# An RWKV layer beside attention with expert weights: a head in another order, and a tail that keeps the last pair's context on the chip

## What is computed

```python
# attention block, per batch b: x is the normalised input
pooled = x.mean(axis=1)
h = relu(pooled @ gw1.T + gb1);  logits = h @ gw2.T + gb2
top_vals, top_idx = top_k(logits, 2);  gates = softmax(top_vals)
# each of q, k, v, o: x @ Wm.T + sum over the 2 experts of gate * (x @ V.T * S) @ U.T + b
attn = softmax(q k^T)            # 16 heads of 8 channels, 1024 tokens
ctx = attn @ v
out = o-projection of ctx
# RWKV block: layer norm, token shift, k/v/r products, a scan over tokens, a second
# norm, and a squared-relu product with a sigmoid gate
```

## Time and profile before

| what | us |
|---|---|
| median of 3 runs | 449.8 |
| lowest and highest | 449.52 and 451.94 |
| the profiled execution | 448.59 |
| span of its trace, first to last instruction | 446.9 |
| busy TensorE | 421.5 |
| busy VectorE | 368.6 |
| busy ScalarE | 345.2 |
| busy GpSimd | 191.0 |

### The profile page before, as it was taken

The page is one execution under the profiler, slowest core; times in us unless marked ns, Lnnn a source line. Parts: engine busy times, 40 slices in busy tenths (PEclk is TensorE's granted clock), DMA queues, the critical chain, the costliest instruction groups (busy, mean ns, idle before and its releaser), DMA issues.

```text
span 446.9 us, 8497 instructions
## 1 busy us (share of the span) xinstructions
PE 421.5 (94%) x3223; PEld 144.1 (32%) x3224; DVE 368.6 (82%) x649; ACT 345.2 (77%) x469; POOL 191.0 (43%) x270
## 2 busy tenths in 40 slices
PE   1889989999999999999999999999999999999993
PEld 1644223333232223232323223323332333322153
DVE  8578899998999997899999789999888999950023
ACT  3547837879887898788799969778986877987862
POOL 5029581935551525282353646416265611321200
PEclk9988999999999999999999999999999999999998
DMA  7004303141414141405141413342422421010314
...
DMA packets 45661, 20.84 MB, mean 47 GB/s; under 512 B 36788, under 2 KB 36916, under 8 KB 45620
## 3 DMA queue, kind: packets, MB, share of 16 engines
...
q10 hardware_dynamic: 838, 0.69, 0.5%
...
## 4 chain that ended last, share of the span: by engine, by line
PE 84%; DVE 9%; ACT 3%; DMA 2%; issue 1%; SPq 0%; DVEq 0%
PE banks L1411 26%; PE banks L1398 22%; PE banks L1321 18%; PE banks L1366 8%; DVE half_max L1134 5%; PE banks L1283 3%; ACT probs L950 3%; PE banks L1289 1%; DMA parts<-ctx_dram 1%; PE banks L1267 1%; PE banks L1218 1%; PE banks L1454 1%; PE banks L1275 1%; PE banks L1184 1%; DVE stats L1002 1%
## 5 line engine op out<-in xcount | busy, mean ns | idle before, releaser
L1134 DVE TENSOR_REDUCE half_max<-banks 128x1 f32<-128x512 f32 x512 | 318.6, 683 | 21.2 <-PE banks L1321 19.6
L950 ACT ACTIVATE probs<-banks 128x1024 f32<-128x1024 f32 x256 | 248.2, 1023 | 47.8 <-PE banks L1398 44.6
L1411 PE MATMUL banks<-probs,v_op 128*32 128x512 f32 x1024 | 136.4, 605 | 0.6 <-ACT probs L950 0.6
L1321 PE MATMUL banks<-k_main,q_main 64*128 64x512 bf16 x512 | 117.6, 388 | 5.6 <-DVE half_max L1134 3.3
L1398 PE MATMUL banks<-q_main,k_main 64*128 64x512 bf16 x512 | 99.3, 377 | 0.4 <-ACT probs L950 0.2
L1398 PE MATMUL banks<-q_tail,k_tail 35*128 35x512 bf16 x512 | 99.3, 377 | 0.0
L1321 PEld LDWEIGHTS banks<-k_main,q_main 64*128 64x128 bf16 x512 | 36.5, 93 | 151.0 <-DVE half_max L1134 132.2
L1398 PEld LDWEIGHTS banks<-q_tail,k_tail 35*128 35x128 bf16 x512 | 27.2, 94 | 25.9
L1398 PEld LDWEIGHTS banks<-q_main,k_main 64*128 64x128 bf16 x512 | 26.4, 95 | 27.0 <-ACT probs L950 12.5
L1411 PEld LDWEIGHTS banks<-probs,v_op 128*32 128x32 f32 x1024 | 20.1, 108 | 32.7 <-issue 30.3
L696 POOL TENSOR_TENSOR work<-work 128x512 f32<-128x512 f32 x16 | 16.6, 1039 | 28.6 <-ACT work L939 28.6
...
## 6 DMA issues: line engine op xcount, KB each, us to landing
...
```

The costliest lines, as they stand in the source:

```text
L950: a.activation(probs[:, (2 * step + h) % 4, :, :], banks[:, 2 * h:2 * h + 2, :], ACT.Exp).then_inc(b_read, 1)
L1134: v.tensor_reduce(half_max[:, n % 2, u:u + 1], ring_bank(at), axis=AX.X, op=ALU.max).then_inc(a_read, 1)
L1321: mm(dst, q_main[HALF * e:HALF * (e + 1), s, P * c:P * c + P], k_main[HALF * e:HALF * (e + 1), s, CHUNK * h:CHUNK * h + CHUNK], start=True ...
L1411: last = mm(banks[g:g + 32, PV_BANK, :], v_op[:, s % 2, step, e, :], probs[:, (2 * step + h) % 4, e, :], start=(step == 0), stop=True, ski ...
```

## The change

In the head the token sums become products with a constant column (`sum_tokens`), the odd chunks are normalised on GpSimd, only batch 0's q and k weights are made at first, and the 22 casts and most of `u_s` move to GpSimd. q and k are split for banks 0 and 2 first; the work for banks 3 and 1 goes between the A units. For pair 0 `place_of` takes the units of the first 512 queries and keys first. In the tail batch 0's contexts are loaded in pair 14, all of batch 1's but the last pair's in pair 15; chunks 0 and 1 are finished inside the loop as ring jobs `out` at steps 122 and 125; the last pair goes from `ctx_sb` straight to TensorE. The reciprocals move from ScalarE to VectorE.

```diff
+FILL_JOBS = {2: [("left", 3, 1), ("project", 1)], 3: [("turn", 1)], 4: [("rows", 3)], 5: [("left", 1, 0)],
...
+OUT_JOBS = {122: 0, 125: 1}
+NORMALISED = {118: 0, 119: 1, 124: 2, 125: 3}
+EARLY = P - 2 * HD
...
+        def place_of(n, u):
+
+            if n == 0 and u < UNITS:
+                return u % 2, u // 2 % 4, u // 8
             return u % 2, u // 4, u // 2 % 2
...
+            load_pair(1, 1)
             load_tails(0, 0)
-            load_pair(1, 1)
             load_pair(2, 2)
...
+            sp.wait_ge(weff_ready, 4)
+            sp.wait_ge(zeros_ok, 1)
+            for e in range(2):
+                for h in range(2):
+                    g = 32 * (2 * e + h)
+                    sp.dma_start(w_last[g:g + HD, h, :], w_eff[EARLY + HD * e:EARLY + HD * (e + 1), 3, 1, :]
+                                 ).then_inc(last_in, 16)
...
+                if step == 0 and p == PAIRS - 2:
...
+                    load_contexts(0, HEADS)
+                if step == 0 and p == PAIRS - 1:
+                    load_contexts(1, HEADS - 2)
...
-            load_contexts(0)
-            store_ctx(PAIRS - 1, SETS - 1)
-            load_contexts(1)
...
+            def normalise(n):
+
+                pool.wait_ge(moments_ready, 4 * n + 4)
+                pool.wait_ge(rstd_ready, n // 2 + 1)
+                for i in range(4 * n, 4 * n + 4):
+                    g.tensor_scalar(xn_tok[:, i, :], x_sb[:, i, :], moments[:, i, 0:1], rstd[:, i:i + 1],
+                                    ALU.subtract, ALU.mult).then_inc(xn_in[1], 1)
...
+            pool.wait_ge(sg_ready, 1)
+            pool.wait_ge(moe_in, 16)
+            for i, b in ((2, 0), (2, 1), (3, 0), (3, 1), (0, 1), (1, 1)):
+                g.tensor_scalar(u_s[:, i, b, :], mat("qkvo"[i] + "U"), sg[:, i, b:b + 1], None, ALU.mult
+                                ).then_inc(us_ready, 1)
...
-            copy_ctx(PAIRS - 1, SETS - 1, (PAIRS - 1) // 2)
-
-            for n in range(CHUNKS):
-                act.wait_ge(attn_in[n], 32)
-                a.activation(den_T[:, n, :], den_T[:, n, :], ACT.Ln).then_inc(den_step, 1)
-                act.wait_ge(den_step, 2 * n + 1)
-                a.activation(den_T[:, n, :], den_T[:, n, :], ACT.Exp, scale=-1.0).then_inc(den_step, 1)
+            act.wait_ge(pv_done, PAIRS * 8)
+            act.wait_ge(ctx_out[1], (PAIRS - 1) // 2 * 16 + 1)
+            a.copy(ctx_sb[:, 1, :].rearrange("c (k p) -> c k p", p=P), token_tiles(bank(PV_BANK))).then_inc(ctx_copied, 1)
...
+            def normalise_ctx(n):
+
+                rows = P if n < 2 else EARLY
...
+                dve.wait_ge(attn_in[n // 2], 64)
+                v.reciprocal(den_T[0:rows, n, :], den_T[0:rows, n, :]).then_inc(recip_ready, 1)
+                dve.wait_ge(recip_ready, n + 1)
...
+            dve.wait_ge(last_den, 1)
+            for i in range(2):
+                at = slice(2 * P * i, 2 * P * (i + 1))
+                v.reciprocal(last_r[:, at], banks[:, 0, at]).then_inc(last_rec, 1)
+            for i in range(2):
+                at = slice(2 * P * i, 2 * P * (i + 1))
+                dve.wait_ge(last_rec, i + 1)
+                v.tensor_tensor(last_T[:, at], ctx_sb[:, 1, at], last_r[:, at], ALU.mult).then_inc(last_ready, 1)
+            add_out(2, bank(2))
+            add_out(3, bank(3))
...
+            def sum_tokens(n):
+
+                b = n // 2
+                pe.wait_ge(xn_in[n % 2], 4 * (n // 2 + 1))
+                for k in range(CHUNK // P):
+                    last = mm(banks[:, 4, 32 + 2 * b:34 + 2 * b], xn_tok[:, 4 * n + k, :], mean_w[:, 0:2],
+                              start=(n % 2 == 0 and k == 0), stop=(n % 2 == 1 and k == 3))
+                return last
...
+                if n == 0 and k == 0:
+                    row_free(0)
+                    row_free(2)
+                elif n == 0 and k == UNITS // 2:
+                    row_free(3)
+                elif n == 0 and k == UNITS:
+                    row_free(1)
...
+                elif name == "out":
+                    pe.wait_ge(rt_ready, 2 * q + 2)
+                    turn_rt(q, dst)
+                    project_ctx(q, dst)
...
+            turn_rt(2, bank(2))
+            turn_rt(3, bank(3))
+            pe.wait_ge(ctx_copied, PAIRS + 1)
+            for g in range(0, P, 32):
+                last = mm(banks[g:g + 32, 0, :], ident[g:g + 32, g + HD:g + HD + 1].to_broadcast([32, 32]),
+                          ctx_sb[g:g + 32, 1, :], start=True, stop=True)
+            last.then_inc(last_den, 1)
+            project_ctx(2, bank(2))
+            project_ctx(3, bank(3))
+            pe.wait_ge(last_in, 64)
+            for n in (2, 3):
+                for k in range(CHUNK // P):
+                    pe.wait_ge(last_ready, k // 2 + 1)
+                    last = mm(bank(n)[:, P * k:P * k + P], last_T[:, P * k:P * k + P], w_last[:, n - 2, :],
+                              start=False, stop=(k == 3))
                 last.then_inc(final_ps, 1)
```

380 lines of the change are left out of this document (217 added, 163 removed).

## The result

The changed kernel takes 453.97 us (median of 4 runs, 453.84 to 456.56), the kernel before 449.66 beside it: 1.0102 times as long, 95% interval 1.0076 to 1.0127. The forecast was 443.5, the range ended at 448.0. The profiled execution has 453.84 us and a span of 452.1, so 5.2 us more than before has to be found in the trace.

| stretch (us) | before | after | difference | forecast |
|---|---|---|---|---|
| to the gate's product | 14.25 | 17.71 | +3.46 | 0 |
| to the first projection | 5.85 | 6.20 | +0.35 | -1.0 |
| to the first A unit | 10.81 | 7.99 | -2.82 | -2.9 |
| opening, to the first scores | 33.72 | 37.50 | +3.78 | +0.6 |
| loop, to the last values' product | 364.30 | 368.01 | +3.71 | +3.7 |

A forecast was written before the change was run, and what follows sets the result against it. In the loop TensorE was taken as the bound, with the head shifting the loop and the tail added. Loop start -3.3, loop +3.7 and tail -6.7 made -6.3 us, from 449.8 to 443.5 us, range 442.0 to 448.0.

The forecast's parts named there:

- signs of being wrong: TensorE idling over 2 us at a time in the opening, 32 x 32 products running serially, or loop over 4 us longer.
- Three terms: Whole kernel: when the loop starts (-3.3 us), what is put into it (+3.7), how long the tail is (-6.7).
- the `out` jobs at 3.7: Loop: two inserted jobs of 1.93 us each, less at most 0.2 hidden, make it 3.7 us longer.
- Token sums: Head: 16 float32 products on TensorE at 0.24 us each, 3.9 us, priced from the o projection's row.
- Term 0: Head, to the gate's product: no gain taken, with bounds of 0.6 us earlier and 0.5 later.
- From the gate to the projection: Head: only one batch of q and k weights wanted, so about 1.0 us less, first projection at 19.1.
- From the projection to the first A unit: Head: 7.9 us in place of 10.8, first A unit at 27.0, 3.9 us earlier.
- the old bubbles were room: Opening: part of 3.2 us of new TensorE jobs fits in three bubbles of 0.88 to 0.98; 34.0 us against 33.4.
- The wait at `rows` 1: Opening: bank 1's third part stands behind `scale_shift(0)`, TensorE stands still 2 us, 1.5 us are lost.
- The rival "slower": Opening: the wait and short products keep the clock at 1.2 GHz through most of it; 452 us, chance 0.05.
- The tail: After the loop: no load in the chain, two 256-column reciprocals at the scan's 0.74 us; 6.7 us less.
- the rival "several passes": Tail: VectorE's reciprocal takes eight times an addition; gain 2.9 us smaller, 446.4, or 448.1 with slower clock; chance 0.33.

The follow-up runs named there:

- e12: e9 with the two `out` jobs inside the loop, as the changed kernel has them; median 447.08 us.
- e9: Changed kernel: VectorE normalises, ScalarE's copies sum tokens, 16 unread warm products before `rows` 1, `out` jobs behind loop, ScalarE reciprocals, denominators' product earlier; ratio 0.9898.
- e4: Changed kernel with the two `out` jobs moved from the loop to the tail; median 452.06 us, ratio 1.0027.
- e6: Changed kernel with 16 warm products, which nobody reads, filling TensorE's wait ahead of `rows` 1 in the opening; ratio 1.0030.
- e1: Changed kernel with all normalising back on VectorE, token sums still on TensorE; median 455.89 us, ratio 1.0100.
- e2: Changed kernel with normalising on VectorE and token sums back on ScalarE's copies, all chunks turned before the gate; median 452.16 us, ratio 1.0047.
- e13: e9 with 36 warm products in the opening in place of 16; 444.06 us, ratio 0.9869.
- e16: e13 with 20 in place of 32 warm products behind the gate's second product; ratio 0.9859.
- e3: Changed kernel with bank 1's third part and spread rows put ahead of `scale_shift(0)` on ScalarE; median 452.53 us, ratio 1.0057.
- e11: Kernel before with 8 and 12 warm products in two waits ahead of the first A product; ratio 0.9994.
- e15: Changed kernel with 36 warm products filling the opening's waits; ratio 1.0002.
- e7: Changed kernel with the last pair's two reciprocals made on ScalarE as Ln and Exp; ratio 1.0039.

## Why the prediction was wrong, step by step

The forecast was -6.3 us and the trace has +5.2, so 11.5 us were missed. Four steps make them up: the token sums 3.5, the way from the gate to the projection 1.35, the opening 3.2, the reciprocals of the tail 3.4. The terms for the loop and for the first A unit held. The prediction's own signs of being wrong lay elsewhere, and none of them came: TensorE idled 1.70 us at most at a time in the opening (2 was the limit), the four 32 x 32 products took 1.03 us and so ran side by side, and the loop grew by 3.71 (4 was the limit).

**What bounds it, and the loop: right.** Three terms, and the `out` jobs at 3.7 (3.71). e12 and e9 show that the jobs cost the same in the tail, once nothing waits there. What the working overlooked: with VectorE's reciprocals something does wait, and the jobs would have been cheaper in the tail (e4: nothing against this profile, 1.5 us against tails at full clock).

**Token sums: the failed step of the head.** 16 products were priced at 0.24 us each, 3.9 in all, from the o projection; they took 6.93, 0.43 each. The count was right and the row was not: it is one at TensorE's full speed, and this early TensorE ran at half of it. The head's turns tell it: four take 1.08 us at 8.35, 1.09 in the kernel before, and 0.66 in the opening at full clock (e6, at 40.69). The sums end at 17.3, ahead of the trace's first record of the clock at 22.4. A narrow product was not cheaper either: 16 instructions of two columns take 3.41 us here, and 16 of 128 columns take 3.47 in the tail at 0.50. No run has the sums at full speed, so what they would cost there is not shown. Term 0, measured +3.46; e1 and e2 show that the sums are it. GpSimd's part was costed at nothing, and rightly so.

**From the gate to the projection.** -1.0 was forecast, +0.35 measured. The halved weight product saved 0.25 (22.90 to 23.91 against 18.84 to 20.10), the chain of single steps around it nothing, and the gate's own chain took 0.60 more (17.71 to 22.90 against 14.25 to 18.84). Over the profiled executions this stretch lies between 5.5 and 7.6 us, more than what was reckoned with. Two profiles have full speed from the gate on: 5.50 in e13, whose first record of the clock begins at 14.1, and 5.85 in the kernel before, at 13.3. So the weights' gain is 0.35 where the speed is the same, and the term of 1.0 was mis-sized; the other 0.7 lost here goes with the later full speed of the changed kernel (22.4), which is read from these profiles and not shown by an experiment.

**From the projection to the first A unit: right.** 7.9 forecast, 7.98 or 7.99 in each kernel with the new head but e16 (8.52).

**The opening: the failed step is that the old bubbles were room.** The wait at `rows` 1 was foreseen with its cause and its 2 us (1.70 + 0.46 measured), and its price of 1.5 was about right (1.3, e3). What failed is the line before it: three old bubbles were taken as room for most of the 3.2 us of new jobs, and they were the fall of the old kernel's own clock: in e11, where it does not fall, VectorE makes 27 reads in a row from 32.97 on without them. At full clock on both sides the old opening takes 31.4 us (e11) and the new one 34.5 to 34.7 (e6, e13, e15), so all of the jobs are paid, and the head's 2.8 is paid back. The fall of the clock costs 3.0 us in the changed kernel (e6) and 2.3 in the kernel before (e11), for stretches of the same length (6.9 and 6.8 us). So of the 3.78 that the opening grew, 3.1 are the jobs and 0.7 the clock.

The rival "slower", at 0.05, had the clock low for 10 to 14 us more than before. In this profile it was low for no longer than before, and the kernel is slower all the same, by the sums' 3.5, the weights' 1.35 and the tail's 3.4 on top of the opening. A rival for a miss by one cause was weighed where the misses of four terms add. That the result lies on its side is not that its mechanism came true.

**The tail: the term mis-sized is the reciprocal.** 0.74 us for 256 columns was taken from the scan's row, 1.73 measured. So the last products start 6.84 us behind the free TensorE instead of 4.93, and at half clock take 3.47 instead of 1.95. This is the rival "several passes", in both of its parts (2.9 and 1.75 reckoned, 1.9 and 1.5 measured). By the rule of the Trainium skill (VectorE: DVE Perf Modes, "Walkthrough: the 8-slice pipeline in each mode") the reciprocal has a repeat count of 8; no rate stands there, and the eightfold price was the prediction's own reading. The trace shows that it is slow, with 6.5 ns for a column against 1.35 for the addition of 512 columns in 0.69 us: a factor of 5 and not 8. e1, e2 and e3 have the same wait and keep the clock (tails of 13.3 us), so the wait's 1.9 is there in every profile with this reciprocal and no filling, and the clock's 1.5 depends on the execution. e7 shows that the reciprocal was the tail's loss: with Ln and Exp on ScalarE the tail takes 11.1 us, and from the free TensorE to the end 10.1, against 10.2 forecast. The rival had the right sign and about three quarters of the size (3.4 of 4.65), and taking the milder row for the forecast was the wrong choice: neither the addition's row (0.42) nor the scan's (0.74) was near the 1.73.
